# Attention of a Flamingo block: row maxima by row-tiled pairs of heads, softmax denominators in six parts, low parts by another engine

## Chip, core and metric

One core of one Trainium2 chip runs the kernel. The metric is the device time of one execution in microseconds (us), lower is better. The engines are PE (TensorE, with its weight loads PEld), DVE (VectorE), ACT (ScalarE), POOL (GpSimd) and SP (SyncE, which issues DMAs).

## What is computed

The block takes x and a context of 4 x 1024 tokens x 512 channels. Cut to what matters:

```python
# attention: 16 heads of 32, q from the normalised x, k and v from the context
q = layernorm(x) rotated by position; k = ctx rotated by position; v = ctx
scores = einsum('bqhd,bkhd->bhqk', q, k) / sqrt(32) + alibi_bias
out = softmax(scores, axis=-1) @ v
x = x + tanh(g_xattn) * out
# gated feed-forward, 512 -> 1536 -> 512, weights and activations rounded to levels
x = x + tanh(g_ffn) * (o(gate, up) @ w_down.T)     # on layernorm(x)
```

A softmax does not change if one number is taken from all scores of a query, so the number only has to be near the row's maximum.

## The kernel before

**Units.** Attention runs over 16 groups `p` of four heads of one batch. A group is two *halves* (`hf`, 32 in all; `qc` says which), 512 queries each against 1024 keys. A half is eight *steps* (`s` 0 to 7), one for each tile of 128 keys. `STEPS` lists all steps, and every engine's program walks through the list in order; the class `Step` says for each step which side work belongs to it. `w = 8*qc + s` numbers the 16 steps of a group.

**A step on PE** (lines 960 to 997). `score` (L934) makes the scores of four heads, 128 keys x 512 queries each, in two PSUM banks in turn. Each is a *group* of four matmuls with 32 output columns of the array, which run side by side. Operands are fp16 pairs: every number is a high and a low part, 32 rows each, so a score needs 96 rows, four rows of bias and one row with the query's maximum (101). `row_max` (L921), running ten steps ahead of the scores, makes the same products with queries on the output partitions: two units of 1024 keys a step, each two groups of four matmuls. Then comes the numerator (L983, fp32, eight matmuls) for the step before, and in three steps of each half the denominators (L956): a matmul of ones with a sum of exponentials. The order is score 0, score 1, three groups of maxima, score 2, one group of maxima, score 3, numerators. In step 1 the denominators stand ahead of the numerators. In step 4 the finished numerators and denominators of the half before are transposed (L993, 128x128 tiles of the array).

**ACT.** `exponent` (L1145) reads a score bank and writes a quarter of a buffer `P` (six in turn). Score n waits for exponential n-2 (`a_exp`), which frees its bank. Between exponentials 1 and 2 of step 1 ACT copies the numerators out (`numT`, L1176), and in step 3 the denominators (`denT`, L1182). The first numerator of a half waits for `numT`. High parts (L1123) come after exponential 3, at w 0 and 2 (queries), 9 and 12 (keys).

**DVE.** It takes the maximum of each unit (L1348); the two pairs of banks `quad[0]`, `quad[1]` are used in turn. After eight steps it transposes 16 columns of maxima into rows, which SP writes into row 100 of `QA`. It makes low parts (L1367) from a copy in PSUM that ACT makes (L1129), and the layer-norm statistics.

**POOL.** It rotates the operands and adds pairs of exponentials into `Ps` (L1936, three in a half). Two more tiles of each half are added to these sums by accumulating DMAs on POOL's queue (L1915). So 8 exponential tiles become 3 sums, and PE makes 3 denominator products.

**SP.** It transposes the stacks of parts `S` into `QA` and `KA` by DMA (L669) when high and low parts are there.

The feed-forward part begins near 911 us. Gate and up products go through DRAM, `gate_d` and `up_d`, as rows of 4096 tokens, of which one transfer moves 128 pieces of 4 KB.

The order on ACT and PE in the code:

```python
exponent(0); exponent(1); [numT copy]; [denT copy]; exponent(2); exponent(3)   # ACT
score(0); score(1); maxima; score(2); maxima; score(3); numerators              # PE
```

Of the kernel before, what the change touches and what calls it, by code (L numbers as in the profile page):

```python
# [15 lines left out]
N = B * T  # L16
# [12 lines left out]
NXL, NWL, NWQ, NP = 7, 4, 2, 6  # L29
# [86 lines left out]
class Step:  # L116


    def __init__(self, g):
# [62 lines left out]
        self.den_out = hf - 1 if s == (2 if hf == NHALF else 3) and 1 <= hf <= NHALF else None  # L182
# [46 lines left out]
def unit_uses():  # L229

    uses = []
    for st in STEPS:
# [4 lines left out]
        if st.low is not None:  # L237
            uses.append(("part", *st.low))
# [25 lines left out]
def den_no(hf, n):  # L264

    return 3 * hf + n + 1


def sum_no(hf, n):

    return 3 * hf + (1, 3, 2)[n]
# [56 lines left out]
class Kernel:  # L328


    def __init__(self, nc, ctx, x, ctx_in, gx, gf, wg, wu, wd, cos_d, sin_d, id_d, bias_d, out):
# [9 lines left out]
        self.gate_d = nc.dram_tensor("gate_scratch", (OT, 128, N), F32).ap()  # L341
        self.up_d = nc.dram_tensor("up_scratch", (OT, 128, N), F32).ap()
# [9 lines left out]
        self.gg = A("gg", [128, 2], F32)  # L352
        self.tg = A("tg", [128, 2], F32)
# [19 lines left out]
        self.tops = A("tops", [128, 1], F32)  # L373
# [14 lines left out]
        self.Pb = [A(f"P{i}", [128, 4, 512], F32) for i in range(NP - 1)]  # L388
        self.bias = nc.alloc_sbuf_tensor_at("bias", [32, T], F32, offset=A.at - 2 * 8192)
        self.biasT = A("biasT", [128, 8, 4, 16], F16)  # L390
        self.Ps = [A(f"Ps{i}", [128, 4, 512], F32) for i in range(3)]
# [4 lines left out]
        self.x2s = A("x2s", [128, 8, 128], F32)  # L396
        self.cm = [A(f"cm{i}", [128, 32], F16) for i in range(2)]
# [26 lines left out]
        self.Pb.append(A("P5", [128, 4, 512], F32))  # L424
# [50 lines left out]
        self.d_acc = [sem(f"d_acc{i}") for i in range(2)]  # L475
# [26 lines left out]
        self.v_rope0, self.v_lo, self.v_max, self.v_cm, self.v_row = sem("v_rope0"), sem("v_lo"), sem("v_max"), sem("v_cm"), sem("v_row")  # L502
# [1507 lines left out]
```

## Time and profile before

| | |
|---|---|
| median of 3 runs | 1801.39 us (1800.41 to 1803.16) |
| the profiled execution | 1800.73 us, its span 1798.9 us |
| first to last step of the scores | 54 to 905 us |
| PE busy | 1605.8 us (89%) |
| DVE busy | 1479.7 us (82%) |
| ACT busy | 1241.8 us (69%) |
| POOL busy | 838.6 us (47%) |

Busy time is the union of an engine's instruction times. A group of matmuls lasts some 0.4 us, but the next starts 0.22 us after it: the pipeline overlaps them. So a busy PE is not one at its peak, and the starts are to be read, not the lengths. The same holds for ACT.

### The profile page before, as it was taken

The page shows a single profiled execution, that of the slowest core. Times are in us where ns is not written, and L with a number is a line of the kernel's source. Part 1 is how long each engine was busy: PE and PEld are TensorE (multiplying, and loading weights), DVE is VectorE, ACT ScalarE, POOL GpSimd, SP SyncE. Part 2 cuts the span into 40 slices and gives each one's busy share as a digit, 9 for nine tenths or more (in the row PEclk, how much of TensorE's full clock was granted, in tenths as well). Part 3 has the DMA queues.
Part 4 walks back from the last instruction along what each step waited for, and adds up shares of the span by engine and source line. Part 5 has one row for each costly group of instructions (what it writes and reads, how often), then busy time and mean ns, then how long its engine had stood idle before and what let it go on. Part 6 is the DMA issues. An engine that isn't in the chain of part 4 may idle for free. (4 is left out here: it accounts for less than half of the span.)

```text
span 1798.9 us, 36886 instructions
## 1 busy us (share of the span) xinstructions
PE 1605.8 (89%) x14777; PEld 633.3 (35%) x14777; DVE 1479.7 (82%) x2116; ACT 1241.8 (69%) x1974; POOL 838.6 (47%) x504
## 2 busy tenths in 40 slices
PE   3899999999999999999869999999999900699999
PEld 0233333333333333333224444444444400344444
DVE  7899999999998898898569989768889998854551
ACT  3688888888889899888723323359986699844440
POOL 5699999999999999998600100200000000000000
PEclk9999999999999999999979999999999955899999
DMA  6688888988888887776649888569973479755551
GB/s 153 151 154 179 167 164 180 177 164 167 163 173 161 171 183 151 163 151 136 139 117 275 242 250 239 203 194 284 280 226 127 139 250 302 237 189 172 176 168 61
DMA packets 344204, 331.73 MB, mean 184 GB/s; under 512 B 214849, under 2 KB 273601, under 8 KB 336097
## 3 DMA queue, kind: packets, MB, share of 16 engines
q1 hardware_dynamic: 335104, 264.37, 55.2%
q0 software_dynamic: 8928, 65.02, 18.3%
q8 instruction: 116, 1.90, 0.4%
q14 instruction: 56, 0.45, 0.1%
HBM read 136.77 MB, written 76.55 MB: 119 GB/s over the span
## 5 line engine op out<-in xcount | busy, mean ns | idle before, releaser
L1348 DVE TENSOR_REDUCE cm<-quad 128x1 f16<-128x1024 f32 x512 | 600.3, 1214 | 63.3 <-PE quad L921 62.3
L1145 ACT ACTIVATE P<-quad 128x512 f32<-128x512 f32 x1024 | 556.8, 598 | 112.3 <-PE quad L934 100.5
L1936 POOL TENSOR_TENSOR Ps<-P,P 128x2048 f32<-128x2048 f32 x93 | 441.0, 4742 | 43.2 <-ACT P L1145 43.1
L934 PE MATMUL quad<-QA,KA 101*32 101x512 f16 x4096 | 365.9, 385 | 6.8 <-ACT P L1145 5.3
L921 PE MATMUL quad<-KA,QA 100*32 100x512 f16 x4096 | 334.7, 391 | 35.6 <-DMA QA<-S 17.8
L983 PE MATMUL quad<-P,cg 128*32 128x512 f32 x2048 | 265.5, 594 | 0.0
L1010 PE MATMUL quad<-x_hl,Wu 128*128 128x512 f16 x1152 | 250.8, 381 | 3.4 <-DMA Wu<-wt_scratch 3.4
L1010 PE MATMUL quad<-x_hl,Wg 128*128 128x512 f16 x1152 | 249.3, 379 | 3.1 <-DMA x_hl<-xs 2.5
L1063 PE MATMUL quad<-Wd,oh 128*128 128x512 f16 x768 | 228.6, 379 | 0.0
L934 PEld LDWEIGHTS quad<-QA,KA 101*32 101x32 f16 x4096 | 105.0, 94 | 298.6 <-ACT P L1145 231.0
L1226 ACT ACTIVATE ev<-quad 128x1024 f32<-128x1024 f32 x96 | 97.3, 1014 | 123.4 <-PE quad L1010 117.3
L921 PEld LDWEIGHTS quad<-KA,QA 100*32 100x32 f16 x4096 | 106.4, 96 | 176.1 <-DVE cm L1348 78.2
L1010 PEld LDWEIGHTS quad<-x_hl,Wu 128*128 128x128 f16 x1152 | 113.0, 98 | 141.0 <-DMA Wu<-wt_scratch 4.3
L1010 PEld LDWEIGHTS quad<-x_hl,Wg 128*128 128x128 f16 x1152 | 112.4, 98 | 140.0 <-issue 5.0
L1618 DVE TENSOR_REDUCE mxt<-ev 128x1 f32<-128x1024 f32 x96 | 116.5, 1214 | 39.6 <-ACT ev L1226 39.3
L1063 PE MATMUL quad<-Wd,ol 128*128 128x512 f16 x384 | 145.5, 379 | 0.0
L1883 POOL TENSOR_TENSOR wq<-wl,wsc 128x512 f32<-128x512 f32 x36 | 43.9, 1221 | 216.5 <-DVE wl L1486 216.5
L1257 ACT ACTIVATE sgm<-gq,qs 128x1024 f32<-128x1024 int16 x96 | 110.0, 1147 | 38.1 <-DVE sgq L1663 36.6
L956 PE MATMUL quad<-Ps,ones 128*32 128x512 f32 x776 | 101.9, 600 | 17.1 <-POOL Ps L1936 7.2
L1759 DVE SCALAR_TENSOR_TENSOR xr<-quad,qs,xr 128x512 f32<-128x512 f32 x32 | 23.9, 750 | 112.3 <-PE quad L1063 108.0
L1063 PEld LDWEIGHTS quad<-Wd,oh 128*128 128x128 f16 x768 | 75.1, 98 | 90.7 <-DVE ol L1738 0.2
L1016 PE MATMUL quad<-ident,column 128*128 128x128 f32 x3 | 1.4, 457 | 110.9 <-DVE column L1421 110.9
(167 smaller groups left out, 2006.3 us busy)
## 6 DMA issues: line engine op xcount, KB each, us to landing
Ps<-P POOLq DMA_DIRECT2D x62, 1024.0 KB, 8.1
gate_scratch<-ev SPq DMA_DIRECT2D x48, 512.0 KB, 3.8
gt<-gate_scratch SPq DMA_DIRECT2D x48, 512.0 KB, 5.8
up_scratch<-ev SPq DMA_DIRECT2D x48, 512.0 KB, 3.4
uf<-up_scratch SPq DMA_DIRECT2D x48, 512.0 KB, 5.1
uf<-up_scratch SPq DMA_DIRECT2D x96, 256.0 KB, 3.6
wt_scratch<-wh SPq DMA_DIRECT2D x72, 128.0 KB, 2.8
xl<-in_x_dram SPq DMA_DIRECT2D x32, 256.0 KB, 5.1
```

What stands on the lines that cost most here:

```text
L921: mm = e.matmul(K.bank(use, c)[j:j + 32, :], K.QA[p % 2][0:100, 4 * qc + qt, h, j:j + 32], K.KA[p % 2][0:100, 4 * c:4 * c + 4, h, :], star ...
L934: mm = e.matmul(K.score[h % 2][j:j + 32, :], K.KA[p % 2][0:101, kt, h, j:j + 32], K.QA[p % 2][0:101, 4 * qc:4 * qc + 4, h, :], start=True, ...
L956: mm = e.matmul(K.den[32 * h:32 * h + 32, :], K.ones[:, :], K.Ps[n % 2 if hf == NHALF - 1 else n][:, h, :], start=n == 0, stop=n == (3 if ...
L983: mm = e.matmul(K.num[32 * h:32 * h + 32, :], K.cg[(p + 1) % 4][:, kt, 32 * h:32 * h + 32], K.Pb[before.g % NP][:, h, :], start=kt == 0, s ...
L1010: mm = e.matmul(K.quad[z][:, 512 * h:512 * h + 512], W(part, c), K.x_hl[:, x, c0:c0 + 512], start=n == 0, stop=n == 11)
L1063: mm = e.matmul(ps, o[k][:, ot, sl], K.Wd[r][:, ot, :], start=ot == m == 0, stop=ot == OT - 1 and m == 2)
L1145: e.activation(K.Pb[pb][:, h, :], K.score[h % 2], ACT.Exp, scale=SCALE / (QPOW * KPOW)).then_inc(K.a_exp, 1)
L1226: e.activation(K.ev[k % NEV][:, :], K.quad[k % 4][:, :], ACT.Copy).then_inc(K.a_ev, 1)
L1257: e.activation(K.sgm[n % NSG][:, :], view(n), ACT.Sigmoid, scale=sg).then_inc(K.a_sig, 1)
L1348: e.tensor_reduce(cm[:, col:col + 1], K.quad[UNIT["max", hm, u] % 2][:, :], AX.X, ALU.max).then_inc(K.v_max, 1)
L1618: e.tensor_reduce(K.mxt[:, col:col + 1], K.ev[k % NEV][:, :], AX.X, ALU.max, apply_absolute_value=True).then_inc(K.v_mx, 1)
L1936: e.tensor_tensor(K.Ps[n][:, :, :], K.Pb[(st.g - 1) % NP][:, :, :], K.Pb[st.g % NP][:, :, :], ALU.add).then_inc(K.g_sum, 1)
```

## The change

Row maxima are made from high parts and bias alone, 36 rows. `S` is laid out anew so that one head of a pair has these in rows 0 to 35 and the other in rows 64 to 99; the two heads' matmuls use the two halves of the array's rows and write to different banks. Each has 128 output columns. Both units of a step stand between score 1 and score 2. DVE reduces a unit to two columns (one for each head, for half of the keys), and once in a half takes the maximum of the two column sets. Scores take all 128 rows.

The accumulating DMAs go. POOL adds two pairs of exponential tiles in a half instead of three, and four tiles are multiplied by the ones directly: six denominator products in a half (the last half keeps its four). They stand after the numerators in steps 3, 4, 5, 7 and, for the half before, 0 and 1. `denT` is copied in step 2. There are seven `P` buffers. Low parts are made by POOL, at w 1 and 7 (queries), 11 and 15 (keys), with no copy by ACT. The high part of queries is two ACT instructions for each half. `gate_d` and `up_d` are stored in contiguous blocks of 512 KB. Further edits follow from these (semaphore counts, buffers, DMA addresses).

```diff
-NXL, NWL, NWQ, NP = 7, 4, 2, 6
+NXL, NWL, NWQ, NP = 7, 4, 2, 7
...
-            elif w in ((10, 14) if p >= 0 else (14, 15)):
-                self.low = (p + 2, 1, w // (14 if p >= 0 else 15))
+            elif w in ((11, 15) if p >= 0 else (14, 15)):
+                self.low = (p + 2, 1, w // 15)
...
-            if w in (1, 6):
-                self.low = (p + 1, 0, w // 6)
+            if w in (1, 7):
+                self.low = (p + 1, 0, w // 7)
...
-        self.sum = (hf, s // 2) if last and s % 2 == 1 else (hf, {1: 0, 4: 2, 7: 1}[s]) if inside and s % 3 == 1 else None
-        self.accumulate = (hf, s // 6, s - 1) if inside and s in (3, 6) else None
+        self.sum = (hf, s // 2) if last and s % 2 == 1 else (hf, s // 4) if inside and s in (1, 5) else None
         self.dens = None
-        if s == 6 and inside:
-            self.dens = (hf, 0)
-        elif s in (1, 2) and 1 <= hf < NHALF:
-            self.dens = (hf - 1, s)
+        if s in (3, 4, 5, 7) and inside:
+            self.dens = (hf, min(s - 3, 3))
+        elif s in (0, 1) and 1 <= hf < NHALF:
+            self.dens = (hf - 1, 4 + s)
...
-        self.den_out = hf - 1 if s == (2 if hf == NHALF else 3) and 1 <= hf <= NHALF else None
+        self.den_out = hf - 1 if s == 2 and 1 <= hf <= NHALF else None
...
+ALONE = {0: 2, 1: 3, 3: 6, 4: 7}
...
-        self.gate_d = nc.dram_tensor("gate_scratch", (OT, 128, N), F32).ap()
-        self.up_d = nc.dram_tensor("up_scratch", (OT, 128, N), F32).ap()
+        self.gate_d = nc.dram_tensor("gate_scratch", (OT, N // GW, 128, GW), F32).ap()
+        self.up_d = nc.dram_tensor("up_scratch", (OT, N // GW, 128, GW), F32).ap()
...
-        for j in range(0, 128, 32):
-            mm = e.matmul(K.bank(use, c)[j:j + 32, :], K.QA[p % 2][0:100, 4 * qc + qt, h, j:j + 32], K.KA[p % 2][0:100, 4 * c:4 * c + 4, h, :],
+        for a in range(2):
+            h, rows = 2 * hp + a, slice(64 * a, 64 * a + 36)
+            mm = e.matmul(K.bank(use, a), K.QA[p % 2][rows, 4 * qc + qt, h, :], K.KA[p % 2][rows, 4 * c:4 * c + 4, h, :],
                           start=True, stop=True)
...
-            if n == 1:
-                e.wait_ge(K.g_sum, sum_no(hf, n))
-            else:
-                e.wait_ge(K.d_acc[n // 2], 16 * hf + 16)
+        elif n in (2, 5):
+            e.wait_ge(K.g_sum, sum_no(hf, n // 5))
+            src = K.Ps[n // 5]
+        else:
+            kt = ALONE[n]
+            e.wait_ge(K.a_exp, score_no(hf, kt, 3))
+            src = K.Pb[(8 * hf + kt) % NP]
         for h in range(4):
-            mm = e.matmul(K.den[32 * h:32 * h + 32, :], K.ones[:, :], K.Ps[n % 2 if hf == NHALF - 1 else n][:, h, :], start=n == 0, stop=n == (3 if hf == NHALF - 1 else 2))
+            mm = e.matmul(K.den[32 * h:32 * h + 32, :], K.ones[:, :], src[:, h, :], start=n == 0, stop=n == last_den(hf))
...
         if st.maxima:
-            row_max(st.hm, 2 * st.im, 0)
-            row_max(st.hm, 2 * st.im, 1)
-            row_max(st.hm, 2 * st.im + 1, 0)
+            row_max(st.hm, 2 * st.im)
+            row_max(st.hm, 2 * st.im + 1)
         if st.inside:
             score(st.hf, st.s, 2)
-        if st.maxima:
-            row_max(st.hm, 2 * st.im + 1, 1)
-        if st.inside:
             score(st.hf, st.s, 3)
-
-        if st.s == 1 and st.dens is not None:
-            denominators(*st.dens)
...
+        numerators(before)
...
-        if st.s != 1 and st.dens is not None:
+        if st.dens is not None:
             denominators(*st.dens)
...
+            dst = K.pairs(w, half)
+            e.activation(dst[:, :, 3:6:2, :], src, ACT.Copy)
+            e.activation(dst[:, :, 0:7:6, :], src, ACT.Copy).then_inc(K.a_hi, 1)
-
-    def copy_part(p, w, half):
-        use = ("part", p, w, half)
-        e.wait_ge(K.g_rope, rope_no(p, w))
-        e.wait_ge(*K.bank_release(use, 0))
-        e.activation(K.bank(use, 0), K.t1[w][:, 4 * half:4 * half + 4, :].rearrange("t i c -> t (i c)"), ACT.Copy).then_inc(K.a_cp, 1)
...
-        e.tensor_reduce(cm[:, col:col + 1], K.quad[UNIT["max", hm, u] % 2][:, :], AX.X, ALU.max).then_inc(K.v_max, 1)
+        e.tensor_reduce(K.cmp[hm % 2][:, c, col:col + 9:8], ps, AX.X, ALU.max).then_inc(K.v_max, 1)
...
+        e.tensor_tensor(K.cm[hm % 2][:, 0:16], K.cmp[hm % 2][:, 0, :], K.cmp[hm % 2][:, 1, :], ALU.max).then_inc(K.v_cmx, 1)
...
+    def low_part(p, w, half):
+        rows = slice(4 * half, 4 * half + 4)
+        src = K.t1[w][:, rows, :].rearrange("t i (k a d) -> t (i k) a d", a=2, d=HD)
+        out, high = K.low_and_high(w, half)
+        e.wait_ge(K.g_rope, rope_no(p, w))
+        e.wait_ge(K.d_st[w][half], stack_no(p - 1))
+        e.wait_ge(K.a_hi, part_no(p, w, half))
+        e.tensor_tensor(out, src, high, ALU.subtract).then_inc(K.g_lo, 1)
...
-        if st.accumulate is not None:
-            hf, n, kt = st.accumulate
-            e.wait_ge(K.a_exp, score_no(hf, kt, 3))
-            e.wait_ge(K.g_sum, sum_no(hf, 2 * n))
-            e.dma_start(K.Ps[2 * n][:, :, :], K.Pb[(8 * hf + kt) % NP][:, :, :], accum_op=ALU.add).then_inc(K.d_acc[n], 16)
+        if st.low is not None:
+            low_part(*st.low)
```

The last `low_part` is in POOL's program, where it comes ahead of a step's rotation and sums.

## Rows read from the trace of the kernel before

**Rows 1.** Busy us: length, PE, PEld, DVE, ACT, POOL; then PEclk, DMA share, GB/s.
```profile
54.00:905.00 851.00, 819.36 (x11072) 284.14 (x11064) 759.55 (x1027) 730.44 (x1366) 781.77 (x423) 1.00 0.82 164
1443.00:1543.00 100.00, 0.67 (x2) 0.40 (x3) 89.67 (x135) 91.89 (x92) 0.00 (x0) 0.50 0.88 281
1560.00:1798.00 238.00, 235.66 (x1092) 106.64 (x1090) 112.74 (x201) 102.72 (x167) 0.00 (x0) 1.00 0.49 158
```

**Rows 2.** Timeline, 278.2 to 281.6 us, all engines: start, length, line and operation.
```profile
277.24 1.05 ACT L1123 ACTIVATE S<-t 128x1024 f16<-128x1024 f32 x1
...
278.24 0.61 PE L934 MATMUL quad<-QA,KA 101*32 101x512 f16 x8
...
278.67 0.82 PE L921 MATMUL quad<-KA,QA 100*32 100x512 f16 x12
278.68 1.09 ACT L1145 ACTIVATE P<-quad 128x512 f32<-128x512 f32 x2 [0.39 <-PE quad L934]
279.33 2.36 DVE L1348 TENSOR_REDUCE cm<-quad 128x1 f16<-128x1024 f32 x2 [0.58 <-PE quad L921]
...
279.33 0.40 PE L934 MATMUL quad<-QA,KA 101*32 101x512 f16 x4
...
279.65 0.60 ACT L1182 ACTIVATE denT<-quad 128x512 f32<-128x512 f32 x1
279.82 0.10 PEld L934 LDWEIGHTS quad<-QA,KA 101*32 101x32 f16 x4 [0.37 <-ACT P L1145]
279.82 0.40 PE L934 MATMUL quad<-QA,KA 101*32 101x512 f16 x4
...
280.04 1.03 PE L983 MATMUL quad<-P,cg 128*32 128x512 f32 x8
...
280.12 1.82 ACT L1145 ACTIVATE P<-quad 128x512 f32<-128x512 f32 x3
...
280.91 0.78 PE L934 MATMUL quad<-QA,KA 101*32 101x512 f16 x8
```

**Rows 3.** Timeline of PE, 274 to 278.4 us: denominators, up to the score at 278.24.
```profile
277.38 1.03 PE L956 MATMUL quad<-Ps,ones 128*32 128x512 f32 x8
```

**Rows 4.** Timeline of PE, 282.8 to 285.6 us: transposes between numerators and scores.
```profile
282.82 1.03 PE L983 MATMUL quad<-P,cg 128*32 128x512 f32 x8
283.78 0.66 PE L993 MATMUL quad<-ident,denT 128*128 128x128 f32 x4
284.27 0.60 PE L993 MATMUL quad<-ident,numT 128*128 128x128 f32 x4
284.80 0.61 PE L934 MATMUL quad<-QA,KA 101*32 101x512 f16 x8
```

**Rows 5.** Waits, 54 to 905 us: who for whom, us in total, times, longest.
```profile
PEld quad L934 <- ACT P L1145: 230.6, 665, 1.0
...
PEld quad L921 <- DVE cm L1348: 58.4, 120, 1.7
...
PEld quad L993 <- DVE cm L1348: 25.3, 30, 0.9
```

**Rows 6.** Groups of instructions, 54 to 905 us: busy us, mean ns, idle before.
```profile
L1145 ACT ACTIVATE P<-quad 128x512 f32<-128x512 f32 x1023 | 556.3, 598 | 112.3 <-PE quad L934 100.5
L1936 POOL TENSOR_TENSOR Ps<-P,P 128x2048 f32<-128x2048 f32 x93 | 441.0, 4742 | 43.2 <-ACT P L1145 43.1
...
L1915 POOL DMA_DIRECT2D Ps<-P x62 | 61.5, 991 | 3.0 <-ACT P L1145 2.4 <-POOL Ps L1936 0.6
...
L1367 DVE SCALAR_TENSOR_TENSOR S<-quad,S 128x512 f16<-128x512 f32 x59 | 40.6, 688 | 4.5 <-ACT quad L1129 3.6
...
L1889 POOL TENSOR_TENSOR wh<-wq,wh 128x512 f16<-128x512 f32 x12 | 20.2, 1686 | 0.0
```

**Rows 7.** Timeline, 269 to 275.2 us: the copy of the numerators in step 1.
```profile
271.97 0.71 ACT L1176 ACTIVATE numT<-quad,tg 128x512 f32<-128x512 f32 x1
```

**Rows 8.** Waits, 1500 to 1565 us: the product pass on its transfers.
```profile
ACT oh L1296 <- DMA uf<-up_scratch: 5.2, 6, 1.7
```

More of the change, by code:

```diff
@@ L396, in __init__ @@
         self.x2s = A("x2s", [128, 8, 128], F32)
+        self.cmp = [A(f"cmp{i}", [128, 2, 16], F16) for i in range(2)]
         self.cm = [A(f"cm{i}", [128, 32], F16) for i in range(2)]
@@ L518, in __init__, with pairs, low_and_high @@
         self.g_wsc, self.g_wdiv, self.g_wlo = sem("g_wsc"), sem("g_wdiv"), sem("g_wlo")
+    def pairs(self, w, half):
+        return self.S[w][:, 4 * half:4 * half + 4, :, :, :].rearrange("t i (k a) n d -> t (i k) (a n) d", a=2)
+    def low_and_high(self, w, half):
+        slots = self.pairs(w, half)
+        return (slots[:, :, 3:6:2, :], slots[:, :, 0:5:4, :]) if w else (slots[:, :, 2:5:2, :], slots[:, :, 0:7:6, :])
     def bank(self, use, half):
@@ L525, in bank_release @@
         n = UNIT[use] - 2
[L526 removed]
+        if n >= 0:
             kind, *a = UNIT_USES[n]
@@ L1105, in key_bias @@
         g = p % 4
-        e.activation(K.S[1][:, :, :, 3, 0:4], K.biasT[:, :, :, 4 * g:4 * g + 4].rearrange("t i n h -> t i h n"), ACT.Copy).then_inc(K.a_kb, 1)
+        for a in range(2):
+            mm = e.activation(K.S[1][:, :, a::2, 1 + 2 * a, 0:4], K.biasT[:, :, :, 4 * g + a:4 * g + 4:2].rearrange("t i n h -> t i h n"), ACT.Copy)
+        mm.then_inc(K.a_kb, 1)
     def high_part(p, w, half):
@@ L1189, in scalar_program @@
             high_part(*st.high)
-        if st.low is not None:
-            copy_part(*st.low)
         for job in st.side:
@@ L1359, in low_part @@
         e.wait_ge(K.a_hi, part_no(p, w, half))
-        if p > 0:
-            e.wait_ge(K.d_st[w][half], stack_no(p - 1))
-        dst = K.S[w][:, rows, :, :, :].rearrange("t i h n d -> t (i h) n d")
-        src = K.t1[w][:, rows, :].rearrange("t i (h d) -> t (i h) d", d=HD)
-        if p > 0:
-            e.wait_ge(K.a_cp, part_no(p - 1, w, half))
-            src = K.bank(("part", p, w, half), 0).rearrange("t (g d) -> t g d", d=HD)
-        e.scalar_tensor_tensor(dst[:, :, 2 - w, :], src, 1.0, dst[:, :, 0, :], ALU.mult, ALU.subtract).then_inc(K.v_lo, 1)
+        src = K.t1[w][:, rows, :].rearrange("t i (k a d) -> t (i k) a d", a=2, d=HD)
+        out, high = K.low_and_high(w, half)
+        e.tensor_tensor(out, src, high, ALU.subtract).then_inc(K.v_lo, 1)
     def centre_x(n):
@@ L1524, in vector_program @@
                 e.tensor_tensor(y, y, K.xg[p % 4][:, 4 * qc:4 * qc + 4, :], ALU.add).then_inc(K.v_x2b, 1)
-        if st.low is not None:
-            low_part(*st.low)
         if st.rows is not None:
@@ L1799, in rope @@
             e.tensor_tensor(K.t1[w][:, :, :], K.t1[w][:, :, :], K.t2[:, :, :], ALU.add).then_inc(K.g_rope, 1)
+    def low_part(p, w, half):
+        rows = slice(4 * half, 4 * half + 4)
+        src = K.t1[w][:, rows, :].rearrange("t i (k a d) -> t (i k) a d", a=2, d=HD)
+        out, high = K.low_and_high(w, half)
+        e.wait_ge(K.g_rope, rope_no(p, w))
+        e.wait_ge(K.d_st[w][half], stack_no(p - 1))
+        e.wait_ge(K.a_hi, part_no(p, w, half))
+        e.tensor_tensor(out, src, high, ALU.subtract).then_inc(K.g_lo, 1)
     e.memset(K.half[:, :], -0.5).then_inc(K.g_half, 1)
```

154 lines of the change are left out of this document (81 added, 73 removed).

## The prediction

> **What bounds the kernel now.** I read the busy times by stretch first. While the scores run, 54 to 905 us, PE, DVE, ACT and POOL are busy for 819, 760, 730 and 782 of 851 us [rows 1]. Four full engines name no bound: busy time hides what a busy engine waits for. So I went to the timeline of single steps, and looked at starts.
>
> The plain step (no denominators, no transposes) that begins with score 0 at 278.24 has its next score 0 at 280.91: 2.67 us [rows 2]. It has two parts. From score 3 (279.82) on, PE runs without a pause: numerators at 280.04, the next score 0 at 280.91, so 0.22 + 0.87 = 1.09 us. The first part, score 0 to score 3, takes 1.58 us, and there the chain is this: exponential 0 starts 0.44 after score 0 (278.68), exponential 1 follows, the two end at 279.77, and 0.05 later the weight load of score 3 starts, which had waited 0.37 us for L1145. Score 3 needs the bank that exponential 1 frees. PE's own work up to there is seven groups at 0.22, 1.54 us: two scores, three groups of maxima, score 2, one of maxima. So two things end within 0.04 us of each other, PE's seven groups and ACT's two exponentials behind a score. The list of waits says the same: the score's weight loads wait for exponentials 665 times, 230.6 us in sum, the longest entry by far [rows 5]. Most of that is hidden under matmuls still in flight, but it shows that the exponentials set the earliest time of these scores. DVE, in contrast, sat idle 0.58 us before this step's maxima [rows 2].
>
> Other steps: one set of denominators adds 0.86 (277.38 to 278.24) [rows 2, 3]. The transposes add 284.80 - 282.82 less the numerators' 0.86, that is 1.12 [rows 4]. A half should then take 8 x 2.67 + 3 x 0.86 + 1.12 = 25.06 us. It takes 851 / 255 x 8 = 26.70 (255 steps lie between first and last score 0 in this stretch, which holds the 256 steps) [rows 1]. The 1.64 us left are stalls: maxima and transposes waiting for DVE (58.4 + 25.3 us in the whole stretch, partly covered; the rest, which I don't split, is denominators waiting for their sums and exponentials held up by other ACT work) [rows 5].
>
> **The maxima.** Four groups of 0.22 a step become two pairs; a pair, if its two matmuls run together, costs one slot of 0.22. PE's work falls by 0.44 us a step, 3.5 in a half. What is it worth on the path? Nothing, by the chain above: score 3 still waits for exponential 1, at 1.58. The cover was exact before and is loose now; PE will idle in it.
>
> There is a new price, the change of the array's tiles before and after the burst. The transposes show such a change [rows 4]: they start at 283.78, 0.07 us before the numerators' end at 283.85, and the scores start at 284.80, 0.07 before the transposes' end at 284.87, while without a change the next group starts 0.18 before the end (279.82 + 0.40 against 280.04) [rows 2]. So a change costs about 0.1. The burst: score 1 at 0.22, first pair at 0.22 + 0.39 - 0.07 = 0.54, second at 0.76, score 2 at 0.76 + 0.32 = 1.08. It came at 279.33, so 1.09, before [rows 2]. Two changes just fit: cost zero. The Trainium skill (TensorEngine Tiling (Array Packing), Key Properties) says that a change of tiling mode drains TensorE, a rule against this edit; the trace agrees, with the 0.1 us at the transposes. The page has no figure for it; by the rows' 0.1 it changes nothing here, and if it were not covered it would be 2 x 0.1 x 256 = 51 us.
>
> **The denominators.** Three sets in a half become six: 3 x 0.86 = 2.58 us. They stand after score 3 and the numerators, where PE has no pause [rows 2, 3]; nothing hides them. This is the term that decides. Sum of the steps by PE: 8 x 2.67 + 6 x 0.86 + 1.12 = 27.64 us for a half.
>
> **ACT.** Two local conflicts appear, both from the new order.
> Step 1: the numerators now come straight after score 3, at 1.80. They wait for numT, which ACT copies after exponential 1. Where the exponentials are on time that slot begins 1.41 after score 0 (denT at 279.65) [rows 2], numT lasts 0.71 [rows 7], so it ends at 2.12, and PE goes on near 2.17: +0.37 a half. Before, the denominators stood ahead and covered this.
> Step 2: it loses its denominators and is a plain step of 2.67 us, but gets denT. In the plain step with denT exponential 2 starts at 280.12, 1.88 after score 0 [rows 2]; two exponentials last 1.09 and one 0.60 [rows 2, 6], so they issue 0.49 apart, and ACT is free at 2.86. At w = 2 the high part of the queries follows, 1.05 us as one instruction [rows 2] and not less as two: 3.91. The next exponential 0 was due at 2.67 + 0.44 = 3.11. It comes 0.8 late and pushes score 3 of step 3. That is in every second half: +0.40 a half. Bounds: 0 if ACT catches up, 0.55 with the second instruction's start-up.
> Rounding of gate weights (12 tiles, at s = 2) and the norms at w = 6: together 0.2, an estimate from their like (0.5 to 0.6 us each where 0.2 are free).
> The copies for the low parts (L1129) that go came after exponential 3, as the high parts do; I count nothing for them, bounds -0.2 and 0 a half.
>
> **DVE and POOL.** DVE loses the low parts, 2 x 0.69 a half [rows 6], and gains one maximum of 16 columns; its bound is 0 to 0.69, and it stands where DVE has slack. Its load, 759.55 / 851 x 26.7 = 23.8 us a half [rows 1], falls to about 22.7 with a half of 29. POOL loses a sum of 4.74 and two issues of 0.99, and gains two low parts; the same operation on weights takes 1.69 [rows 6]. -3.3 us a half; its queue also no longer holds the DMAs. Both get slack, so most of the 1.64 us of old stalls go. The low part stands ahead of the rotation and the sum on POOL, and waits for ACT's high part of the step before; behind it waits SP's transpose, due two or more steps (5 us) later, so nobody is late. I keep 0.35 us of stalls (DVE's 3.5 us steps with statistics next to plain steps, late norms), with bounds of 0 and 1.64.
>
> **The rest.** Start-up: maxima alone run there, paced by DVE's 1.18 us a unit (2.36 for two [rows 2]), unchanged; more and smaller memsets, 0 to +2. The contiguous blocks: the pieces stay 4 KB. The down products are PE's (235.7 of 238 us) and cannot gain; the product pass waits 5.2 us for transfers [rows 1, 8]. So -5 to 0; I take -1.
>
> **The sum.** 27.64 + 0.37 + 0.40 + 0.20 + 0.35 = 28.96 us a half, 2.26 more than 26.70. The extra sets belong to 31 halves: +70.1. With -1 and +0.5: 1800.7 + 69.6 = 1870.3 us. The profiled execution is 0.7 below the median of the runs, so I say 1871.
>
> **The rivals.**
> - *The pairs do not run together* (the change does not do what it says). For: no row shows two row tiles; the groups of four in the trace are column tiles. Then four matmuls take 0.54 to 1.20, score 2 comes at 1.52, score 3 at 1.74 instead of 1.58: +0.16 x 256 = 41, so 1912. The Trainium skill (same page, Key Properties) has tiles executing in parallel; no row here shows it for row tiles. It speaks against this rival.
> - *DVE was the pacer, and the kernel gets faster.* For: DVE is busy 89%, maxima waited 58.4 us for it. If a half followed DVE's load at the same share, it would take 22.7 / 0.893 = 25.4 us: -1.3 x 31, 1761. It decides if denominators only fill pauses that PE had. Against: the plain step runs in 2.67 with DVE idle 0.58, and no pause stands after score 3.
> - *All stalls vanish*: 27.64 a half, +29, so 1829. For: every engine but PE is relieved. Against: the two conflicts on ACT are written in its order.
> - *POOL's low parts are late.* If the strided form takes twice 1.69 and SP's transposes behind it wait, a group may lose 2 us more: 15 x 2 = 30, so 1900. For: POOL was full. Against: it loses 3.3 us a half.
>
> **How the numbers follow.** Forecast 66% (1845 to 1895); pairs in series 12% (around 1912); stalls vanish 8% (1825 to 1845); low parts late 5% (1900); faster 9% (around 1761). The bounds of the unknown terms: 27.64 gives +29; 27.64 + 0.37 + 0.55 + 0.2 + 1.64 = 30.4 gives +115. The range 1828 to 1914 leaves out the faster case, half of the serial one and some edges: about 2 in 10. A measurement of this kernel can tell about 0.2% (3.6 us) from no change. Slower 0.89, same 0.02, faster 0.09.
>
> **What the changed profile would show.** Score 0 to score 3 still near 1.58 us, with PE idle before score 2 or 3 and the maxima in two slots 0.22 apart; if the pairs are serial, four. Denominator sets in six steps at 0.86 each with no wait on POOL or DMA. Numerators of step 1 waiting for numT by 0.3 to 0.4. Exponential 0 of step 3 late in even halves. PE's busy time in the scores' stretch at a lower share, DVE's under 85%, POOL's well under 90%; the stretch 920 instead of 851 us. The forecast is wrong if score 3 comes clearly before 1.58, if denominators start under other work, or if the clock granted to PE (1.00 now [rows 1]) falls in the pauses.

## The result, and the profile after

| | before | after |
|---|---|---|
| median | 1801.99 us | 1991.74 us (1990.54 to 1997.72) |
| profiled span | 1798.9 us | 1990.3 us |
| ratio | | 1.106, 95% interval 1.1036 to 1.1084 |

The change makes the kernel 190 us slower. I had forecast slower, but by 70 us, and 1991.7 lies 78 us above the upper end of the range.

The busy times by stretch come first, as in [rows 1]. The first line is the stretch of the scores, then the product pass and the down products.

```profile
54.00:1105.00 1051.00, 911.88 (x8824) 256.62 (x8822) 848.24 (x996) 698.02 (x1345) 649.55 (x387) 0.95 0.31 70
...
1640.00:1740.00 100.00, 5.96 (x22) 2.55 (x23) 90.87 (x139) 93.24 (x96) 0.00 (x0) 0.51 0.88 288
1755.00:1990.00 235.00, 232.06 (x1076) 105.00 (x1073) 109.11 (x194) 99.45 (x160) 0.00 (x0) 1.00 0.48 156
```

From the first to the last step of the scores the kernel after takes 1054.3 us where the kernel before took 849.3, 205 us more, and the loss is all there: from the last score on, it is 12 us faster (881.6 against 893.9 us). PE's busy share falls from 96% to 87% though it has more to do, and the granted clock is 0.95 where it was 1.00.

The next view is the table of the page that groups instructions by line (busy us, mean ns, idle before). These rows answer [rows 6].

```profile
L1360 DVE TENSOR_REDUCE cmp<-quad 128x2 f16<-128x1024 f32 x512 | 601.3, 1220 | 175.5 <-PE quad L939 174.8
...
L1958 POOL TENSOR_TENSOR Ps<-P,P 128x2048 f32<-128x2048 f32 x62 | 282.4, 4555 | 171.9 <-ACT P L1162 171.9
...
L1368 DVE TENSOR_TENSOR cm<-cmp 128x16 f16<-128x16 f16 x32 | 122.8, 3837 | 1.1
```

The third row is what I had bounded by 0.69 us: the maximum that merges the two partial maxima (the *merge* from here on). It writes 16 columns and takes 3.84 us, more than three times the 1.22 us in which DVE reduces 1024 columns.

Why so long? The timeline around one of them shows it (start, length, engine, line and operation, idle before). First POOL and DVE:

```profile
436.62 4.54 POOL L1958 TENSOR_TENSOR Ps<-P,P 128x2048 f32<-128x2048 f32 x1 [1.43 <-ACT P L1162]
...
437.29 3.89 DVE L1368 TENSOR_TENSOR cm<-cmp 128x16 f16<-128x16 f16 x1
...
441.10 2.35 POOL L1815 TENSOR_TENSOR t<-t,t 128x1024 f32<-128x1024 f32 x1
441.21 0.89 DVE L1373 STREAM_TRANSPOSE crow<-cm 32x32 f16<-32x32 f16 x4
442.04 2.31 DVE L1360 TENSOR_REDUCE cmp<-quad 128x2 f16<-128x1024 f32 x2
```

POOL's running sum ends at 441.16, DVE's merge at 441.18. In 31 of the 32 halves the merge ends 0.02 to 0.03 us after a POOL sum, in the first one 0.02 us after a POOL rotation. So it does not compute for 3.84 us. It waits for POOL to finish. Then PE, in the same timeline:

```profile
440.10 0.60 PE L951 MATMUL quad<-QA,KA 128*32 128x512 f16 x8
...
443.28 0.50 PE L939 MATMUL quad<-KA,QA 36*128 36x512 f16 x2 [2.57 <-DVE cmp L1360]
...
444.94 1.05 PE L951 MATMUL quad<-QA,KA 128*32 128x512 f16 x8
...
445.77 1.93 PE L987 MATMUL quad<-P,cg 128*32 128x512 f32 x8
...
449.18 1.07 PE L951 MATMUL quad<-QA,KA 128*32 128x512 f16 x8
...
450.19 0.61 PE L939 MATMUL quad<-KA,QA 36*128 36x512 f16 x4
```

The next maxima find their bank still occupied, because DVE had not read it. PE stands for 2.57 us, and score 2 comes 4.84 us after score 0 (440.10 to 444.94) instead of 1.09. A second price follows: after this pause the same eight numerator matmuls take 1.93 us, where they take 1.03 at full clock [rows 2]. The granted clock is at its lower level there (the view by stretch; the last columns are PEclk, DMA share, GB/s):

```profile
446.00:447.00 1.00, 1.00 (x8) 0.19 (x4) 1.00 (x2) 0.70 (x2) 1.00 (x1) 0.50 0.06 16
```

It fell at 443.4, after PE had stood from 440.7 to 443.3, and rose again at 450.3. From the first to the last score it is at 0.50 in 24 such pieces, 113 us together; in the kernel before, in none.

The last row of PE's timeline answers the question about pairs: four maxima matmuls in 0.61 us, as two slots. The two matmuls of a pair start within 3 ns of each other, the pairs 0.24 us apart.

The starts of score 0 (its fourth matmul) give the whole account. Mean length of each step of a half, in us, over all halves (with `reduce`, the first experiment below):

```
step       0     1     2     3     4     5     6     7     sum
before    3.00  4.18  3.49  2.71  3.91  2.72  3.77  2.85  26.63
after     3.66  3.93  2.66  4.03  4.63  3.51  2.66  8.12  33.20
reduce    3.52  3.93  2.67  4.04  4.63  3.51  2.66  3.61  28.57
```

Steps 0 to 6 sum to 25.08 us in the kernel after. One step in eight, the one in which the maxima wait for a DVE held up by the merge, holds the surprise.

### The profile page after: what moved, and what is told of

The parts are those of the page before. It is cut to its first block and busy times, and to the rows that moved or that the text cites. A ratio compares the mean times of both kernels' runs of the same rounds, so it can differ in the third digit from the quotient of the medians.

```text
span 1990.3 us, 32116 instructions
## 1 busy us (share of the span) xinstructions
PE 1691.5 (85%) x12449; PEld 605.5 (30%) x12449; DVE 1571.4 (79%) x2092; ACT 1212.5 (61%) x1962; POOL 711.3 (36%) x471
## 5 line engine op out<-in xcount | busy, mean ns | idle before, releaser
L1360 DVE TENSOR_REDUCE cmp<-quad 128x2 f16<-128x1024 f32 x512 | 601.3, 1220 | 175.5 <-PE quad L939 174.8
L951 PE MATMUL quad<-QA,KA 128*32 128x512 f16 x4096 | 371.6, 399 | 35.0 <-ACT P L1162 15.9
L1958 POOL TENSOR_TENSOR Ps<-P,P 128x2048 f32<-128x2048 f32 x62 | 282.4, 4555 | 171.9 <-ACT P L1162 171.9
L987 PE MATMUL quad<-P,cg 128*32 128x512 f32 x2048 | 283.8, 632 | 5.5 <-ACT numT L1193 5.5
L939 PE MATMUL quad<-KA,QA 36*128 36x512 f16 x1024 | 171.4, 400 | 130.8 <-DVE cmp L1360 112.4
L951 PEld LDWEIGHTS quad<-QA,KA 128*32 128x32 f16 x4096 | 108.0, 97 | 397.7 <-ACT P L1162 260.6
L976 PE MATMUL quad<-P,ones 128*32 128x512 f32 x992 | 148.5, 678 | 0.0
L1368 DVE TENSOR_TENSOR cm<-cmp 128x16 f16<-128x16 f16 x32 | 122.8, 3837 | 1.1
L1908 POOL TENSOR_TENSOR wq<-wl,wsc 128x512 f32<-128x512 f32 x36 | 37.8, 1050 | 217.4 <-DVE wl L1501 217.4
L939 PEld LDWEIGHTS quad<-KA,QA 36*128 36x128 f16 x1024 | 33.5, 94 | 258.0 <-DVE cmp L1360 155.9
```

The costliest lines, as they stand in the source:

```text
L939: mm = e.matmul(K.bank(use, a), K.QA[p % 2][rows, 4 * qc + qt, h, :], K.KA[p % 2][rows, 4 * c:4 * c + 4, h, :], start=True, stop=True)
L951: mm = e.matmul(K.score[h % 2][j:j + 32, :], K.KA[p % 2][:, kt, h, j:j + 32], K.QA[p % 2][:, 4 * qc:4 * qc + 4, h, :], start=True, stop=True)
L976: mm = e.matmul(K.den[32 * h:32 * h + 32, :], K.ones[:, :], src[:, h, :], start=n == 0, stop=n == last_den(hf))
L987: mm = e.matmul(K.num[32 * h:32 * h + 32, :], K.cg[(p + 1) % 4][:, kt, 32 * h:32 * h + 32], K.Pb[before.g % NP][:, h, :], start=kt == 0, s ...
L1360: e.tensor_reduce(K.cmp[hm % 2][:, c, col:col + 9:8], ps, AX.X, ALU.max).then_inc(K.v_max, 1)
L1368: e.tensor_tensor(K.cm[hm % 2][:, 0:16], K.cmp[hm % 2][:, 0, :], K.cmp[hm % 2][:, 1, :], ALU.max).then_inc(K.v_cmx, 1)
```

## The experiments

Theory A: the merge is held up because it reads two operands from SBUF while POOL is at work; an instruction with one such operand would pass. Rival B: the merge is slow in itself, or the wait belongs to the new order of work. All ratios are to the kernel before, whose median lay between 1799.8 and 1802.0 us. Where one time stands without a ratio (three versions), it is a single execution.

**The merge with one input.** The same 16 maxima, from one operand of 32 columns:

```
-        e.tensor_tensor(K.cm[..][:, 0:16], K.cmp[..][:, 0, :], K.cmp[..][:, 1, :], ALU.max)
+        e.tensor_reduce(K.cm[..][:, 0:16], K.cmp[..][:, :, :].rearrange("q c n -> q n c"), AX.X, ALU.max)
```

> The changed kernel, with the one DVE instruction that merges the two sets of maxima (L1368, two inputs in SBUF, 3.84 us, ending in 31 of 32 cases 0.03 us after POOL's sum) replaced by a reduction of the same numbers, which reads one input. Theory A, DVE's second read of SBUF waits until POOL's running instruction has ended: the instruction takes 0.2 to 0.3 us, step 7 of a half falls from 8.1 to about 3.5 us, a half from 33.2 to about 28.6, PE's clock stays at 1.00, and the time is 1990 - 31 x 4.6 = about 1848 us. Theory B, what is slow is the place or the semaphore ahead of it, not the kind of instruction: it stays at 3.8 us and the time at 1990 us. Of the original forecast's steps, this leaves denominators, numT and denT conflicts and the transfers: about +58 us for the scores less some 12 us for what follows, against the kernel before.

Measured: 1844.3 us, ratio 1.0236 (1.0219 to 1.0253). The merge's row in the view of its tile (shortest/median/longest in ns), and the stretch of the scores:

```profile
L1368 DVE TENSOR_REDUCE cm<-cmp x31: 185/188/190, 73.9 to 932.4; 128x16 f16<-128x32 f16 x31
```
```profile
54.00:960.00 906.00, 861.51 (x8820) 248.03 (x8812) 735.50 (x995) 697.81 (x1342) 651.18 (x387) 1.00 0.37 82
```

188 ns instead of 3837, the clock back at 1.00, step 7 back at 3.61 us. In 31 of the 32 halves the reduction starts 0.66 to 0.67 us into a POOL sum, as the merge did, and takes the same 188 ns. This one line is 147 us of the 190: 32 x 3.65 = 117 us of holding, and 30 us that I do not split further, the low clock among them.

**POOL's sum at another time.** The merge stays with two inputs; POOL's second sum of a half comes one step later:

```
-  self.sum = ... (hf, s // 4) if inside and s in (1, 5) else None
+  self.sum = ... (hf, s // 4) if inside and s in (1, 6) else None
...
```

> The changed kernel with POOL's second sum of a half one step later (step 6 instead of 5), so that it no longer runs when DVE merges the maxima; the merging instruction is untouched. Theory A: it takes under 0.3 us where POOL is idle and, where POOL's rotation or addition is running then, lasts until that ends (at most 2.4 us); mean well below 3.8, time 1850 to 1920 us. Theory B (place or semaphore): 3.8 us still, about 1990 us.

Measured: 1853.6 us. The merge in the same view, and from the timeline one instance beside POOL:

```profile
L1368 DVE TENSOR_TENSOR cm<-cmp x31: 233/252/3903, 76.3 to 940.6; 128x16 f16<-128x16 f16 x31
```
```profile
107.11 2.38 POOL L1815 TENSOR_TENSOR t<-t,t 128x1024 f32<-128x1024 f32 x1
...
109.22 0.29 DVE L1368 TENSOR_TENSOR cm<-cmp 128x16 f16<-128x16 f16 x1
```

The same instruction takes 252 ns in the median, and 3903 in the one half where it still meets a sum. Here it met the rotation instead, which ends at 109.49, and ended itself at 109.51. It is not slow; what POOL is doing sets its end: all 32 end 0.02 to 0.03 us after a POOL instruction.

**Inputs of 32 bits.** Are two 16-bit inputs special? The partial maxima go into 32-bit buffers. SBUF has no room left for new ones, so two tiles of the feed-forward part, free at that time, hold them:

```
-  self.cmp = [A(f"cmp{i}", [128, 2, 16], F16) for i in range(2)]
+  self.cmp = [t[:, 0:32].rearrange("p (c n) -> p c n", c=2) for t in (self.mxt, self.mxs)]
```

> The changed kernel with the maxima of a unit kept as 32-bit numbers (in a tile of the feed-forward part that is free then), so that the merging instruction has two 32-bit inputs in SBUF instead of two 16-bit ones. Theory A1, any two inputs in SBUF make it wait for POOL's running instruction: still 3.8 us, ending 0.03 us after POOL's sum, time about 1990 us. Theory A2, only the fast mode for 16-bit numbers needs what POOL holds: 0.1 to 0.3 us and about 1846 us.

The page's groups by line:

```profile
L1368 DVE TENSOR_TENSOR cm<-mxs 128x16 f16<-128x16 f32 x16 | 62.9, 3933 | 0.5
L1368 DVE TENSOR_TENSOR cm<-mxt 128x16 f16<-128x16 f32 x16 | 59.5, 3717 | 0.5
```

1996.9 us: nothing changes. The width of the inputs does not count.

**Is it the kind of instruction?** The merge with one input is also another operation, a reduction instead of a `tensor_tensor`. The trace of the kernel before separates the two. It has a DVE `tensor_tensor` with one input in PSUM and one in SBUF (view of the tile):

```profile
L1520 DVE TENSOR_TENSOR x2s<-quad,rdn x32: 690/692/693, 99.6 to 917.1; 128x512 f32<-128x512 f32 x32
```

In 23 of the 32 cases a POOL instruction runs from before its start to past its end, and it never takes longer than 693 ns. So it is the second input from SBUF that makes DVE wait.

**The same instruction in the kernel before.** One maximum of 16 columns with two SBUF inputs a half, its result unused:

```
         e.wait_ge(K.v_max, max_no(hm, 15))
+        e.tensor_tensor(K.twin[:, :], K.cm[hm % 2][:, 0:16], K.cm[hm % 2][:, 0:16], ALU.max)
```

> The kernel before with one more DVE instruction a half, a maximum of 16 columns with two 16-bit inputs in SBUF, ahead of the transposes of the maxima (its result isn't used). Theory, any two-input DVE instruction waits for what POOL runs: POOL is busy 92% of this stretch, so it lasts until POOL's instruction ends, 1 to 4 us each, never ends in the middle of one of POOL's sums, and the time rises by 31 x 1 to 4 us, 1830 to 1920 us. Rival, the wait comes from something else that the change brought (low parts on POOL, the new layout): 0.1 to 0.3 us each, 1801 to 1810 us.

The view of the tile:

```profile
L1353 DVE TENSOR_TENSOR twin<-cm x32: 166/1316/2870, 48.9 to 978.9; 128x16 f16<-128x16 f16 x32
```

1904.5 us, 103 us above the kernel before, for 32 instructions. The first, with POOL idle, takes 166 ns; each of the 31 others ends 0.02 to 0.03 us after an instruction of POOL. So rival B falls: the order of the change isn't needed for it. That two SBUF inputs make DVE wait for POOL is shown: with one input, at another time, with another width, and in another kernel.

**The layout alone.** Contiguous blocks in the scratch tensors, on the kernel before:

```
-  self.gate_d = nc.dram_tensor("gate_scratch", (OT, 128, N), F32).ap()
+  self.gate_d = nc.dram_tensor("gate_scratch", (OT, N // GW, 128, GW), F32).ap()
...
-  e.dma_start(dst_d[ot, :, 1024 * cp:1024 * cp + 1024], ...)
+  e.dma_start(dst_d[ot, cp, :, :], ...)
```

> The kernel before with nothing but the contiguous blocks for gate_d and up_d. In the changed kernel, from the last score on, 12 us are gone: the up products take 248.8 instead of 254.2 us and the product pass 87.6 instead of 92.4. Theory A, that is the work of the blocks: about 1801.8 - 11 = 1791 us (1788 to 1794), the scores' stretch unchanged at 851 us. Rival, it comes from what attention leaves behind (queues, buffers, another start): 1799 to 1802 us.

1792.1 us, ratio 0.996 (0.9947 to 0.9974): 7.6 us faster than the kernel before (1799.7 beside it), and the fastest version of this study by its median. The page's list of transfers (KB each, us to landing) for this version:

```profile
gt<-gate_scratch SPq DMA_DIRECT2D x48, 512.0 KB, 5.4
up_scratch<-ev SPq DMA_DIRECT2D x48, 512.0 KB, 3.0
uf<-up_scratch SPq DMA_DIRECT2D x48, 512.0 KB, 4.4
```

Before, the same three rows of the page say 5.8, 3.4 and 5.1 us.

**Denominators ahead of numerators in step 1**, on the version with the one-input merge:

```
+        if st.s == 1 and st.dens is not None:
+            denominators(*st.dens)
         numerators(before)
...
-        if st.dens is not None:
+        if st.s != 1 and st.dens is not None:
```

> e1_reduce with the denominators of step 1 ahead of the numerators, as in the kernel before. Theory, the numerators of step 1 wait for numT (step 1 is 3.91 instead of 3.53 us): step 1 falls by 0.37 us, 31 x 0.37 = 11.5 us, 1844 to about 1833 us. Rival, the wait only moves to another place: within 3 us of e1_reduce.

1834.3 us (ratio 1.0179, 1.0166 to 1.0192), 10 us under the version without it. Step 1 falls from 3.93 to 3.56 us and no other step moves. 0.37 us is the very term that I had given to the numerators' wait for numT.

**Back to fewer denominators.** The forecast priced three more sets at 80 us and found nothing to set against them. Then the one-input merge with the old sums (three sums on POOL, two accumulating transfers, three sets) should give some 1761 us:

```
+  self.accumulate = (hf, s // 6, s - 1) if inside and s in (3, 6) else None
...
-  return 6 * hf + n + 1
+  return 3 * hf + n + 1
```

> The changed kernel with the merging reduction of e1_reduce and with the sums, accumulating transfers and three denominator products of the kernel before. It keeps the half-array maxima, POOL's low parts and the contiguous blocks. Theory A, denominators are added to PE's path in full and the halved maxima give only the old stalls back: a half takes 25.06 us and 0.5 to 1 us of stalls, 28 us less than before in the scores' stretch, and with 12 us less in what follows about 1761 us; against e1_reduce it is 31 x 2.6 = 80 us less. Rival, denominators are hidden: within 10 us of e1_reduce. Rival, the maxima's 0.44 us a step of PE are worth their full size: 31 x 3.5 = 109 us less than before, near 1680 us.

Missed: 1835.0 us, ratio 1.0201 (1.0165 to 1.0238). The number is the one that the rival of hidden denominators named (within 10 us of 1844), but its mechanism is not seen: plain steps take 2.66 to 2.67 us in the median here too, and the medians of the steps sum to 26.27 us against 28.28 with six sets. Yet 14 of the 31 halves take 28 to 33 us. POOL is busy 817 of 846 us, the granted clock is 0.98, and PE waits for POOL's sums (who for whom, us in total, times, longest):

```profile
PEld quad L978 <- POOL Ps L1967: 35.8, 24, 3.4
PE quad L978 <- POOL Ps L1967: 28.1, 15, 3.2
```

Three variants between the two plans, all with the one-input merge. Four sets, with two sums and two accumulating transfers (tile 2 in step 3, tile 6 in step 7):

> e1_reduce with two accumulating transfers a half (tile 2 onto the first sum, tile 6 onto the second) and so four denominator products instead of six, in steps 5, 7, 1 (ahead of the numerators) and 2, with denT in step 3 as before. POOL keeps two sums. Theory, each set of denominators costs 0.86 us of path, and numT and denT are covered again: 8 x 2.67 + 4 x 0.86 + 1.12 = 25.9 us a half and 0.4 of stalls, 26.3: 13 us less than before in the scores' stretch, 11 less after it, about 1778 us. Rival, the sets cost less than that or accumulating transfers cost elsewhere: 1800 to 1835 us. If POOL is the bound again as in e5_oldsums (busy 49 to 50 of 50 us, products waiting for sums), 1820 or more; with one sum less it should be busy near 80%.

Three sets, with a third accumulating transfer:

> As e7_four, with a third accumulating transfer (tile 3 onto the first sum, after tile 2): three products a half, all in steps 0 to 2 of the next half, POOL still with two sums. Theory: 8 x 2.67 + 3 x 0.86 + 1.12 = 25.06 us and 0.5 of stalls, 25.6: 34 us less than before in the scores' stretch, 11 less after it, about 1757 us. Rival, POOL waits in its queue for the first transfer before it issues the second, or the last step waits for sums: as e7_four or slower, 1780 to 1800 us.

Four sets, with sum and transfer one step earlier (tile 5 in step 6):

> e7_four with the second sum of a half made of tiles 3 and 4 (POOL, step 4) and its accumulating transfer (tile 5) issued in step 6 instead of 7; denominator products in steps 6, 7, 1 and 2. In e7_four the products waited 70 us for that transfer, most of it in four late groups, while the medians of its steps sum to 26.25 us a half, 0.4 of it such a wait. Theory, the transfer was late by less than a step (3.5 us): the waits go, a half takes 26.0 us on average, and the time is 1802 - 31 x 0.7 - 8 = about 1773 us, 1765 to 1785. Rival, what waits is the load of the DMA engines, not the time of issue: as e7_four, 1805 to 1820 us.

```
               median    (range)             ratio (95%)
four sets      1816.4  (1807.1 to 1823.0)   1.0103 (1.0068 to 1.0138)
three sets     2195.3  (2162   to 2216)     1.2082 (1.1996 to 1.2169)
earlier        1815.1  (1793.8 to 1825.8)   1.0061 (1.0036 to 1.0085)
```

All three missed their theory; the first and the third fell where their rivals had them, the second missed by 438 us. There the transfers of steps 6 and 7 are issued some 3 us apart. A transfer lands after 10.8 us in the median, 34 of the 93 take over 13 us, the longest 39.5, and PE waits (in the longest of the four executions):

```profile
PE quad L981 <- DMA Ps<-P: 255.4, 33, 18.3
...
PEld quad L981 <- DMA Ps<-P: 135.7, 15, 16.5
```

**Is it POOL's load?** If so, cutting POOL's low parts must help the version with the old sums, and do nothing in the changed plan, where POOL has slack:

```
-  e.tensor_tensor(out, src, high, ALU.subtract)
+  e.tensor_tensor(out[:, 0:4], src[:, 0:4], high[:, 0:4], ALU.subtract)
```

> The version with three sums and two accumulating transfers a half, the merge as a reduction, and POOL's low parts cut to 4 of their 16 groups of columns (the low parts of the keys and queries are therefore wrong; only the time is read). It asks what made that version take 1835.0 us instead of about 1765. Theory P (POOL is too full): POOL there was busy for the whole stretch; its low parts last 1.59 us x 2 a half. At a quarter of the columns they take about 0.4 each, POOL gets 2.4 us a half back, and the halves of 28 to 32 us come down towards the 26.3 of their steps' medians: 1835 - 31 x (1.5 to 2.4) = 1761 to 1790 us. Rival T (the transfers are what is late, and POOL's load does not matter): POOL idles more, PE waits as long for sums and transfers, 1825 to 1837 us.

> The changed kernel with the merge as a reduction (1844.3 us), and POOL's low parts cut to 4 of their 16 groups of columns (wrong low parts; only the time is read). POOL has slack here (it waits 107 us for exponentials before its sums, from 54 to 900 us), so its low parts should cost nothing: both theories say 1842 to 1846 us. If it comes out under 1838, the move of the low parts to POOL has a price of its own in the new plan too, and the forecast's zero for it was wrong.

The edit cuts less than I had planned. The dimension that it cuts has 8 groups for a low part, not 16, so half of the columns remain, not a quarter: the traces show 128x256 instead of 128x512, and 1.04 instead of 1.59 us in the first version, 0.68 instead of 1.17 in the second. The other half of the low parts is left out.

The second version gave 1846.9 us (ratio 1.0265), a little over the expected window and no faster: half of the low parts' work is worth nothing in the changed plan. The first fell on neither side: 1879.1 us (1.0431, 1.0396 to 1.0466), slower by 44 us with less work. So a third thing was at play, and its trace shows it (of the longest of five executions, 1913.2 us). Of 62 accumulating transfers, 7 took 20.6 to 34.2 us to land instead of 8.1 in the median. Four of the seven were issued within 0.05 us of a stacking transpose, the other three were the next transfer behind such a one. The cleanest case is in the version "earlier", with one late pair. POOL, SP and PE there:

```profile
319.03 0.89 POOL L1951 DMA_DIRECT2D Ps<-P  x1
```
```profile
319.00 2.16 SPq L692 DMA_TRANSPOSE KA<-S  x1
324.18 0.39 SPq L661 DMA_DIRECT2D cg<-in_ctx_dram  x1
324.73 34.01 SPq L692 DMA_TRANSPOSE KA<-S  x1
```
```profile
329.98 1.03 PE L994 MATMUL quad<-P,cg 128*32 128x512 f32 x8
351.41 1.08 PE L983 MATMUL quad<-Ps,ones 128*32 128x512 f32 x4 [20.39 <-DMA Ps<-P]
```

The transfer issued at 319.03 lands 32.3 us later, at 351.4, where PE goes on (two of the expectations below have shorter landing times, 27.5 and 20 to 29 us; these are the traces'). The next transpose holds SP's queue for 34 us, PE stands for 20.4 us, and the half takes 51.7 us instead of 27. Leaving out the version "three sets", no other transfer in these versions was issued within 0.1 us of a transpose, and none but those took over 13.0 us. Where the transpose leads by 0.4 to 0.5 us, the transfer takes 9.7 to 11.8 us.

"Three sets" does not fit so well: of its 34 late transfers, eight were issued within 0.16 us of a transpose (15 to 27 us), the other 26 were not. So nearness to a transpose is not the only thing that makes these transfers late.

**Keeping the two apart.** One wait, in SP's program, so that the first transpose of a group stays behind the transfer:

```
             e.wait_ge(K.pe_score, score_no(2 * (p - 2) + 1, 7, 3))
+            if (w, half) == (1, 0):
+                e.wait_ge(K.d_acc[1], 16 * (2 * p - 3) + 16)
```

> The version with two accumulating transfers and four sets of denominators (1815.1 us, and varying by 32 us), with one wait added: the first stacking transpose of a group waits until the accumulating transfer of the same step has landed. In the profile of that version the only late transfer (27.5 us to land instead of 7.7) was issued at 319.03, within 0.1 us of a stacking transpose (319.00), and the half around it took 51.7 us instead of 27. Theory C (the coincidence is the cause): 1812.8 - 24.7 = 1788 us, between 1782 and 1795, runs within 6 us of each other, no transfer over 12 us; the wait itself is free, since these stacks are read a half (26 us) later. Rival R (late transfers come at random, or from the fuller DMA engines): 1805 to 1820, and varying as before.

> The same added wait in the version with three sums, two accumulating transfers and low parts of a quarter (1879.1 us; low parts wrong, only the time is read), where 7 of 62 transfers took 20 to 29 us, every first one of a series issued within 0.1 us of a stacking transpose. Theory C: the late ones go, the halves are those that were undisturbed there (26.1 to 29 even, 25.1 to 30 odd): 1785 to 1825 us, thus 55 us or more faster. Rival R: 1865 to 1890.

> The same added wait in the version with three sums, two accumulating transfers and whole low parts (1835.0 us). Its profile had one transfer of 12.6 us issued 0.1 us from a transpose and four of 8.5 to 10.3 close behind one; the rest of its loss was PE waiting for POOL's sums (64 us). Theory C with POOL as the bound: 1815 to 1832 us, only a little faster, and PE still waits for the sums. If it falls to 1800 or less, POOL was late because of these transfers, not because of its load.

"Earlier" with the wait: 1797.0 us (1789.2 to 1804.5), ratio 0.9977 (0.996 to 0.9994), 18 us under itself, and the longest landing is 10.3 us. The median lies 2 us above the window, and the executions still spread over 15 us, more than I expected; the profiled one, with a span of 1787.4 us, is the fastest of the twelve. "Old sums" with half of the low parts: 1825.0 us (1.0136), 54 us less, and no transfer takes over 11.1 us. "Old sums" with whole low parts: 1837.4 us (1.0203), 5 us above its window and unchanged, PE still waiting for POOL:

```profile
PEld quad L980 <- POOL Ps L1969: 36.8, 24, 3.7
PE quad L980 <- POOL Ps L1969: 29.7, 18, 3.4
```

So the collision is real and expensive where the order of work brings it about (18 and 54 us), and POOL's load is a cost of its own (1837 against 1825 us with less work on it). The kernel before shows no late transfer: the longest of its 62 took 10.9 us, and no transpose is issued within 0.9 us of one.

## Why the prediction was wrong, and where it was right

- **The step that failed** is the sentence on DVE: "gains one maximum of 16 columns; its bound is 0 to 0.69, and it stands where DVE has slack". The 0.69 came from [rows 6], L1367, an instruction `S<-quad,S`: one input from PSUM, one from SBUF. The new one has two from SBUF, and no row that I had taken shows such an instruction beside a busy POOL. What I priced as work of its own was a wait for POOL. The same group of rows has POOL's longest instruction, 4.74 us, and that should have been the upper bound: 32 x 4.74 = 152 us above the forecast, 2023 us. And slack was not the question: 3.84 us in one place made PE late, and that cost more than the 1 us a half by which DVE's load had fallen. The price, with its consequences, is 147 us.
- **The trace of the kernel before had a sign of it**, which I overlooked. The low parts of the first group read two operands from SBUF. Three of these four instructions run with POOL idle and take 0.68 to 0.69 us; the fourth starts while a POOL instruction runs (37.98 to 39.28), and takes 1.06:

```profile
37.98 1.30 POOL L1789 TENSOR_TENSOR t<-cg,sin 128x512 f32<-128x512 f32 x1
38.77 1.06 DVE L1367 SCALAR_TENSOR_TENSOR S<-t,S 128x512 f16<-128x512 f32 x1
```

- **The Trainium skill has this rule** (SBUF — State Buffer, Terms and "SBUF: two separate sides"): DVE and GpSimd share a pair of ports as an exclusive lock, held for a whole instruction, and a DVE instruction with two SBUF inputs is among those that need it, when GpSimd's instruction reads SBUF. The traces agree: POOL's instructions here read SBUF, the ends are 0.02 to 0.04 us apart, and it takes 188 ns with one input. That it is a lock on ports is the skill's account; the runs show the wait. I read the row for its size and did not ask where its operands lie.
- **The remaining plan**: with that one line changed the kernel takes 28.57 us a half, against a forecast of 28.96, and 1844.3 us against 1871. Between the forecast's span (1868.5) and the measured one (1843.3) lie 25.2 us: 8.5 in the stretch of the scores (+61.6 instead of +70.1), 13.6 behind the last score (-14.6 instead of -1), 3.1 ahead of the first (51.5 instead of 54.2, where I had +0.5).
- **The sum by PE** (27.64) holds. Step 6 and step 2 are plain steps and take 2.66 and 2.67; steps 0, 5 and 7 with a set of denominators take 3.52, 3.51 and 3.61 for 3.53; step 4, with set and transposes, 4.63 for 4.65.
- **Maxima in pairs, worth nothing**: right in this plan (plain steps take 2.66 to 2.67 us, as the 2.67 before). Score 2 comes 1.08 to 1.09 after score 0 in steps 0 to 2, so the two changes of the array's tiles are just covered, and score 3 waits for exponentials at 1.58. The rival with pairs in series falls with L939's 0.61 us for four.
- **Step 1**: 0.40 measured (3.93 less 3.53), 0.37 forecast, and taken away by the exchange of denominators and numerators.
- **Step 3**: denT and the queries' high part together cost 4.04 - 3.53 = 0.51 on average; 0.40 forecast, 0.55 the bound. The 0.2 for gate weights and norms and the 0.35 of kept stalls are not seen: 27.64 + 0.40 + 0.51 = 28.55.
- **POOL**: "gets slack" is right in the changed plan (650 of 1051 us; low parts cut to half change nothing). The rival of late low parts falls.
- **Transfers, -1 us**: wrong in size and outside its bounds of -5 to 0. The layout alone is worth 7.6 us. It leaves some 5 to 7 us of the 12 and 15 behind the last score without a cause that I could name. "The pieces stay 4 KB" was an argument from the size of pieces, where the landing times are what counts.
- **DVE as the pacer, faster kernel**: falls. Denominators fill no pauses; they cost their 0.86 each.
- **The clock**: I named a fall of the granted clock as a sign against me, and it fell, to 0.95, from a cause I had not on my list.
- **What the forecast left out on the other side**: it charged 80 us for three sets and credited the accumulating transfers with nothing. The versions that keep them show that they are not free under the new order: 1815 and 1835 us, where the sum of the steps says 1761 to 1778. Only with the added wait does one of them pass the kernel before, by 0.2%, and it contains the contiguous blocks, which alone bring 0.4%. So nothing in the rest of the change has been shown to gain.

Left open: why the best of these still varies by 15 us between executions, what else delays the transfers of "three sets", and whether the maxima in pairs alone, without moving the low parts, are worth anything on the kernel before. The latter was not tried.

## What to carry to other kernels

Price a new DVE instruction by where its operands lie, not by its columns: with two inputs from SBUF and a busy POOL, it lasts until POOL's instruction ends (3.84 us here), and a reduction over one strided operand computes the same without waiting (0.19 us). Bound an operation that no row shows by the longest thing it can wait for, and look at who waits behind it at that place. A new order of work can bring transfers of two queues together that were apart before; where the trace shows both late, give them an order with a wait (18 and 54 us here).

## What the runs showed of the hardware

- A DVE maximum of 16 columns takes 166 ns with POOL idle, 3.9 us when it starts 0.67 us into a POOL sum of 4.56 us, with inputs of 16 or 32 bits; a reduction with one SBUF input takes 188 ns at the same place. 32 of them cost 103 us in the kernel before and 147 in the kernel after (against the form with one input).
- An accumulating transfer of 1 MB within SBUF lands in 8.1 us in the median (6.8 to 10.9 in the kernel before); issued within 0.05 us of a stacking transpose it took 28.0 to 34.2 us in all five cases of two versions, and in four of the five the next transpose then held SP's queue for over 30 us; at 0.15 us it took 13.0 in "old sums". What makes both crawl is not shown, and "three sets" has late ones that no transpose is near.
- Changing the array's tiles costs about 0.1 us each way, as the transposes showed before [rows 4]: in the kernel after, the first maxima start 0.32 us behind score 1, and score 2 starts 0.33 us behind the last pair (437.65 to 437.97, 438.20 to 438.53), where groups without a change follow after 0.22. Two row tiles of the maxima run together: four matmuls in 0.61 us.
- POOL's own instructions do not always take the same time: a sum 4.56 us in the changed plan and 4.79 with the old sums, a low part 1.17 and 1.59. I have no cause for that.
